# A transformer block on one core: new order of stages, scores in two pieces, first norm's weights applied in the copy

## Chip, cores and metric

One core of one Trainium2 chip. The metric is the device time of one execution in microseconds (us), as the median of several runs. The engines are called TensorE (PE, with its weight loads as PEld), VectorE (DVE), ScalarE (ACT), GpSimd (POOL) and SyncE (SP, which here only issues DMAs).

## What is computed

The input is 4 sequences of 2048 tokens with 256 features, float32. Cut to what matters:

```python
x  = x + attn(layernorm(x))            # attn is a pre-norm block of its own
x  = x + experts(layernorm(x))

attn(q_x): xn = ln1(q_x)               # mean, variance, times ln1_w, plus ln1_b
  q, k, v = xn @ wq + bq, xn @ wk + bk, xn @ wv + bv    # 16 heads of 16
  fq, fk = elu(q) + 1, elu(k) + 1
  kv  = einsum("bhnd,bhne->bnde", fk, v)     # per token: over the HEADS
  qkv = einsum("bhnd,bnde->bhne", fq, kv)
  qk  = einsum("bhnd,bnd->bhn", fq, fk.sum(heads))
  x   = q_x + (qkv / (qk + 1e-6)) @ wo + bo
  x   = x + gelu(ln2(x) @ fc_w + fc_b) @ proj_w + proj_b    # 256 -> 1024 -> 256

experts(x): gates from the mean of a sequence (top 2 of 8, softmax)
  out = sum over chosen e of gate[e] * gelu(x @ expert_w[e].T + expert_b[e])
```

The attention mixes the 16 heads of one token with each other, not tokens. The kernel does it as scores between all heads of 4 tokens at a time (a 64x64 block), times a mask that keeps pairs of the same token, times the values.

## The kernel before

The work is cut into 16 **tiles** of 512 tokens, four to a sequence. No engine is scheduled by a planner: the function `iterations` (line 58) yields, for iteration 0 to 23, a list of **stage** names, and each engine walks the same lists and issues, in that order, its own part of each stage. So one list sets five in-order queues at once, and an instruction that waits holds back everything behind it on its engine, DMA issues included. `LAG` (line 43) gives how many iterations behind the newest tile a stage works. In the steady state an iteration handles five different tiles.

The stages that matter, by iteration i:

- `L`: SP loads tile i. `DS`, `D1`: DVE statistics and normalisation of tile i into `xhat` (the reciprocal root is POOL's, line 418). `X`: PE transposes `xhat` (L827) and ACT copies it to `xhT` (L458). `DV`, `DQ`, `DK`: PE multiplies with the value, query and key weights (L871, eight matmuls each); ACT takes exp and relu (L480, L481), DVE joins them to features (L650), SP stores them (L326). Values are stored by ACT's own DMA queue (L473), which waits first until the values of the tile before have been read back.
- `VL`: SP reads the values of tile i-1 back in another layout, 16 DMAs (L339); `VT` transposes them (PE L879, ACT L488). `K0`, `K1`: SP reads queries and keys of the first and of the second half of a tile, 8 DMAs each (L351). `B0`: PE scores of the first half (L890, 128 matmuls of 16x64), and DVE's mask (L657).
- `M1` to `M4`: four rounds of the 256-1024-256 network of tile i-3 (up-projection L933, gelu L503 and L504, rest L670, down-projection L917) merged with attention of tile i-2. `M1` multiplies the scores of the first half with the values (L902), and ACT evicts to `ot` (L511). `M2` holds the scores of the second half, `M3` their product with the values. `M2` and `M4` on SP each do two things: they store half of `ot` to `scratch_nd` (L357), wait for that to land, and load it back as numerator and denominator (`nd`, L362). `B1` to `B4` are the same without the network, `C1` to `C4` the network alone.
- `N0`, `N`: DVE divides the two halves (reciprocal L686), and `N` splits the result into `hT` (L696, L697). `A2`: PE output projection (L977, 24 matmuls), DVE adds and takes statistics (L707 and on). `R`: DVE normalises to `hn` (L596). `H`: PE transposes `hn` (L827) for the network; the copies are ACT L492 and DVE L677.
- `J7`, `JA`: last down-projection and its sum. `Y`, `YB`: the residual's part. `XS`, `XL`: SP stores and reloads the network's result. `F1`, `F3`: PE runs the two chosen experts (L839), `F4` joins them, `FX` is a branch for a third, `F2` transposes the sum (L1021), adds (L803) and stores (L380). `G`: the gate of a sequence, once in four tiles (L991).
- Head only: `W1` folds the first norm's weight and bias into the query, key and value weights (PE L846, DVE L622 and L625), and ACT begins only when that is done. `WS` folds the second norm's and splits the weights of three products into two float32r parts each (DVE, lines 630 to 642).

`TAIL` (line 46) is the second part of an iteration from 7 on, `MERGED` (line 49) its first. Iterations 3 to 6 use `EARLY` (line 50), whose second part already has `A2` ahead of `DK`:

```python
TAIL = ["DV", "DQ", "DK", "A2", "F1", "R", "F3", "F4", "SA", "H", "B0", "FX", "F2"]
MERGED = ["L", "XS", "VL", "K0", "M1", "J2", "Y", "M2", "K1", "DS", "Z", "M3", "D1", "M4", "N0"]
```

## Time and profile before

| what | value |
|---|---|
| median of 3 runs | 1129.65 us (1126.64 to 1133.05) |
| the profiled execution's own time | 1129.7 us |
| its span in the trace | 1127.8 us |
| PE busy | 974.4 us (86%), 12232 matmuls |
| DVE, ACT, POOL busy | 58%, 43%, 16% |
| mean granted PE clock | 0.916 of full speed |
| chain that ended last | PE 48%, SP's queue 13%, DVE 12%, issue 12%, DMA 10% |

PE is busy most of the span, but not evenly: in 40 slices its busy tenths are 5 7 5 4 7 at the start and 9 or 8 through the middle. The clock column shows 1.0 as full speed and 0.5 as half: 2.4 and 1.2 GHz. A matmul that runs at half clock counts as busy for twice as long, so a busy PE can still lose time.

### The profile page before, as it was taken

What the parts mean: (1) busy time and instruction counts of PE and PEld (TensorE: products, weight loads), DVE (VectorE), ACT (ScalarE), POOL (GpSimd) and SP (SyncE); (2) the same over time, 40 slices, a digit from 0 to 9 for tenths busy, and PEclk for the clock granted to TensorE, in tenths of its full rate; (3) what the DMA queues carried; (4) which work ended last, traced back from release to release, by engine and by line L of the source; (5) the groups of instructions that cost most, each with busy time, mean ns of one, the idle gap of its engine ahead of it and who ended that gap; (6) DMA issues with size and microseconds to landing.
All of it is one profiled execution on the core that took longest, in us unless ns stands there. A gap on an engine that the chain in (4) does not pass through costs nothing.

```text
span 1127.8 us, 29248 instructions
## 1 busy us (share of the span) xinstructions
PE 974.4 (86%) x12232; PEld 736.0 (65%) x12232; DVE 654.8 (58%) x1564; ACT 486.3 (43%) x770; POOL 185.2 (16%) x113
## 2 busy tenths in 40 slices
PE   5754798989898899999999899999999899797966
PEld 3342676767676758685777668586866768585723
DVE  1263566667665665765656766656656664657433
ACT  1413354535353444545363454445453455152422
POOL 1020121212121211212111211212111210202000
PEclk9858798989898899999998999989999999798989
DMA  4556255454545435546364545546364544241123
GB/s 179 114 96 136 42 124 99 119 103 115 100 119 101 115 76 141 114 114 140 96 147 91 137 86 120 108 116 138 94 140 94 134 98 98 53 122 39 38 74 113
DMA packets 360343, 120.88 MB, mean 107 GB/s; under 512 B 325520, under 2 KB 342160, under 8 KB 359952
## 3 DMA queue, kind: packets, MB, share of 16 engines
q1 hardware_dynamic: 353552, 108.47, 42.9%
q10 hardware_dynamic: 6656, 10.50, 2.7%
q8 instruction: 98, 1.61, 0.6%
q14 instruction: 37, 0.30, 0.1%
HBM read 60.20 MB, written 58.72 MB: 105 GB/s over the span
## 4 chain that ended last, share of the span: by engine, by line
PE 48%; SPq 13%; DVE 12%; issue 12%; DMA 10%; POOL 3%; ACT 1%; ACTq 1%; DVEq 0%; POOLq 0%
PE pw L933 10%; PE pj L917 8%; DMA scratch_nd<-ot 5%; SPq L339 5%; PE ps L871 5%; PE ps L890 5%; SPq L351 5%; PE pw L839 4%; PE pj L839 4%; PE ps L977 3%; DMA nd<-scratch_nd 3%; PE ps L902 2%; PE pw L871 2%; DVE nd L686 2%; SPq L362 2%
## 5 line engine op out<-in xcount | busy, mean ns | idle before, releaser
L933 PE MATMUL pw<-hT,w_fc 128*128 128x512 f32 x768 | 219.1, 428 | 9.6 <-DVE hT L677 9.6
L917 PE MATMUL pj<-w_pj,hidden 128*128 128x256 f32 x1536 | 215.6, 291 | 2.7 <-DVE hidden L670 2.7
L917 PEld LDWEIGHTS pj<-w_pj,hidden 128*128 128x128 f32 x1536 | 203.9, 196 | 14.1 <-DVE hidden L670 3.7
L670 DVE TENSOR_TENSOR hidden<-xhT,hidden 128x512 fp32r<-128x512 f32 x128 | 88.5, 691 | 206.8 <-ACT hidden L504 206.0
L503 ACT ACTIVATE xhT<-pw,col 128x512 f32<-128x512 f32 x128 | 88.0, 688 | 252.9 <-PE pw L933 251.6
L933 PEld LDWEIGHTS pw<-hT,w_fc 128*128 128x128 f32 x768 | 151.1, 208 | 42.5 <-DVE hT L677 11.5
L871 PE MATMUL ps<-xhT,w_qkv 128*128 128x512 f32 x256 | 125.5, 636 | 3.4 <-ACT xhT L458 3.2
L657 DVE TENSOR_TENSOR am<-ps,mask 128x512 f32<-128x512 f32 x128 | 79.4, 683 | 41.5 <-PE ps L890 41.5
L890 PE MATMUL ps<-kq 16*64 16x64 f32 x4096 | 81.9, 311 | 21.9 <-issue 19.7
L890 PEld LDWEIGHTS ps<-kq 16*64 16x64 f32 x4096 | 74.4, 209 | 35.5 <-issue 35.5
L686 DVE RECIPROCAL nd<-nd 128x256 f32<-128x256 f32 x32 | 56.0, 1749 | 64.1 <-DMA nd<-scratch_nd 64.1
L871 PEld LDWEIGHTS ps<-xhT,w_qkv 128*128 128x128 f32 x256 | 51.2, 207 | 62.0 <-issue 57.4
L504 ACT ACTIVATE hidden<-pw,col 128x512 fp32r<-128x512 f32 x128 | 87.5, 684 | 0.0
L511 ACT ACTIVATE ot<-ps,den_eps 128x512 f32<-128x512 f32 x64 | 69.7, 1197 | 38.3 <-PE ps L902 37.5
L977 PE MATMUL ps<-w_o,hT 128*128 128x256 f32 x384 | 55.9, 306 | 34.0 <-DVE hT L697 34.0
L977 PEld LDWEIGHTS ps<-w_o,hT 128*128 128x128 f32 x384 | 51.6, 207 | 45.5 <-DVE hT L697 26.9
L650 DVE SCALAR_TENSOR_TENSOR fqk<-elu 128x512 f32<-128x512 f32 x64 | 42.9, 688 | 54.1 <-ACT elu L481 54.1
L424 POOL TENSOR_TENSOR x<-x,row 128x1024 f32<-128x1024 f32 x16 | 37.6, 2351 | 222.3 <-DVE x_sb L722 219.5
L839 PE MATMUL pw<-zT,w_e 128*128 128x512 f32 x128 | 59.6, 609 | 8.4 <-DMA b_e<-in_eb 7.7
L418 POOL TENSOR_TENSOR rs<-var,mhalf 128x8 f32<-128x8 f32 x16 | 27.8, 1740 | 215.1 <-DVE var L611 209.5
L839 PE MATMUL pj<-zT,w_e 128*128 128x512 f32 x128 | 57.8, 594 | 5.5 <-DVE out_sb L803 5.5
L871 PE MATMUL pw<-xhT,w_qkv 128*128 128x512 f32 x128 | 57.8, 594 | 0.7 <-ACT vb L488 0.7
(109 smaller groups left out, 1187.9 us busy)
## 6 DMA issues: line engine op xcount, KB each, us to landing
scratch_nd<-ot SPq DMA_DIRECT2D x32, 512.0 KB, 4.1
nd<-scratch_nd SPq DMA_DIRECT2D x96, 128.0 KB, 2.7
x_sb<-in_x SPq DMA_DIRECT2D x16, 512.0 KB, 5.9
scratch_v<-feat_v ACTq DMA_DIRECT2D x16, 512.0 KB, 2.9
scratch_q<-fqk SPq DMA_DIRECT2D x32, 256.0 KB, 3.6
scratch_k<-fqk SPq DMA_DIRECT2D x32, 256.0 KB, 4.7
vd<-scratch_v SPq DMA_DIRECT2D x256, 32.0 KB
kq<-scratch_q SPq DMA_DIRECT2D x128, 64.0 KB, 2.7
```

The source lines that it names most:

```text
L503: nc.scalar.activation(gelub[:, u], pw[u], ACT.Gelu, bias=b_fc[:, m:m + 1])
L504: nc.scalar.activation(hidden[:, m % SLOTS, 0], pw[u], ACT.Gelu, bias=b_fc[:, m:m + 1]).then_inc(S[f"pw_free{u}"], 1)
L511: nc.scalar.activation(dst[:, r // 2, v], src, ACT.Identity, bias=den_eps[:, :]).then_inc(S[f"sa_free{v}"], 1)
L657: last = nc.vector.tensor_tensor(am[:, j].rearrange("p (k n) -> p k n", n=BLOCK), ps[:, j].rearrange("p (k n) -> p k n", n=BLOCK), mask[:, ...
L670: nc.vector.tensor_tensor(hidden[:, m % SLOTS, 1], gelub[:, u], hidden[:, m % SLOTS, 0].bitcast(f32), ALU.subtract).then_inc(S["rest_ready ...
L686: link(nc.vector.reciprocal(d, d))
L839: last = nc.tensor.matmul(bank, w[:, c, P * m:P * (m + 1)], zT[:, p.t % RING, c], start=(c == 0), stop=(c == NC - 1))
L871: last = nc.tensor.matmul(bank, w_qkv[:, j // NC, c, P * (j % NC):P * (j % NC + 1)], xhT[:, c], start=(c == 0), stop=(c == NC - 1))
L890: last = nc.tensor.matmul(ps[BLOCK * v:BLOCK * (v + 1), j, BLOCK * k:BLOCK * (k + 1)], kd[rows, b, cols], qd[rows, b, cols], start=True, s ...
L917: last = nc.tensor.matmul(pj[u][:, D * s:D * (s + 1)], hidden[:, m % SLOTS, a, lo:lo + P], w_pj[:, b, m], start=(m == 0 and n == 0 and s = ...
L933: last = nc.tensor.matmul(pw[bank], w_fc[:, b, c, P * m:P * (m + 1)], hT[:, a, c], start=(n == 0), stop=(n == len(order) - 1))
L977: last = nc.tensor.matmul(sb2[u][:, D * s:D * (s + 1)], attnT[:, a, c, lo:lo + P], w_o[:, b, c], start=(c == 0 and n == 0), stop=(c == NC ...
```

## The change

Five edits, all in the order of the work but one:

1. **First norm.** `W1` is gone. ACT's copy of `xhT` applies `ln1_w` as scale and `ln1_b` as bias, per partition.
2. **First tiles.** Iterations 0 to 2 have new lists: statistics of tile 1 and 2, and `D1`, run an iteration earlier; `WS` comes ahead of `DV` of tile 1; `K0` comes ahead of `VL`.
3. **Scores in two pieces.** `scores(b)` becomes `scores(b, part)` of 64 matmuls each. `B0` is split in `B0` and `B8`, with `H` and `F3` between them in iterations 7 to 15; in `M2` the pieces stand ahead of and behind the down-projection.
4. **SP.** Store and reload of `ot` are stages of their own: `NS0`, `NL0`, `NS1`, `NL1`. `VL` moves behind `NS0`, `K0` behind `NL0`, `K1` behind `NL1`.
5. **Tail.** `A2` moves between `DQ` and `DK`, `R` ahead of `F1`, `H` (norm's transposes) between `F1` and `F3`.

```diff
-TAIL = ["DV", "DQ", "DK", "A2", "F1", "R", "F3", "F4", "SA", "H", "B0", "FX", "F2"]
+TAIL = ["DV", "DQ", "A2", "DK", "R", "F1", "B0", "H", "F3", "F4", "SA", "B8", "FX", "F2"]
...
-MERGED = ["L", "XS", "VL", "K0", "M1", "J2", "Y", "M2", "K1", "DS", "Z", "M3", "D1", "M4", "N0"]
-EARLY = ["L", "VL", "K0", "M1", "Y", "M2", "K1", "DS", "M3", "D1", "M4", "N0", "X", "J7", "JA", "YB", "VT", "N",
-         "DV", "DQ", "A2", "R", "DK", "SA", "B0", "H"]
+MERGED = ["L", "XS", "M1", "J2", "Y", "NS0", "VL", "M2", "NL0", "K0", "DS", "Z", "M3", "NS1", "D1", "M4", "NL1", "N0", "K1"]
+EARLY = ["L", "M1", "Y", "NS0", "VL", "M2", "NL0", "K0", "DS", "M3", "NS1", "D1", "M4", "NL1", "N0", "K1", "X", "J7", "JA", "YB",
+         "VT", "N", "DV", "DQ", "A2", "R", "DK", "SA", "B0", "B8", "H"]
...
-    yield 0, ["DS:0", "L:1", "D1", "W1", "X", "DV", "DQ", "DK"]
-    yield 1, ["DS", "D1", "VL", "K0", "K1", "X", "DV", "DQ", "DK", "L:2", "WS", "VT", "B0"]
-    yield 2, ["VL", "K0", "DS", "D1", "Y", "B1", "X", "DV", "B2", "K1", "DQ", "B3", "B4", "N0", "VT", "DK", "YB", "N",
-              "A2", "R", "SA", "B0", "H"]
+    yield 0, ["DS:0", "L:1", "D1", "X", "DV", "DS:1", "DQ", "L:2", "D1:1", "DK"]
+    yield 1, ["X", "K0", "WS", "VL", "DV", "DQ", "DS:2", "DK", "D1:2", "B0", "B8", "VT", "K1"]
+    yield 2, ["K0", "VL", "Y", "B1", "NS0", "X", "DV", "B2", "NL0", "DQ", "B3", "NS1", "VT", "NL1", "N0", "K1",
+              "DK", "YB", "N", "A2", "R", "SA", "B0", "B8", "H"]
...
-                if p.stage in ("B2", "M2", "B4", "M4"):
-                    half = int(p.stage[1]) // 2 - 1
+                if p.stage in ("NS0", "NS1", "NL0", "NL1"):
+                    half = int(p.stage[2])
                     part = slice(HALF * half, HALF * (half + 1))
+                if p.stage in ("NS0", "NS1"):
                     for u in range(2):
                         wait(f"sa_free{u}", at(f"sa_free{u}"))
                     sp.dma_start(nd_dram.rearrange("j e h t -> (j e) h t")[:, :, part], ot[:, :, part]).then_inc(S["nd_out"], 16)
+                if p.stage in ("NL0", "NL1"):
                     wait("attnT_ready", at("attnT_ready"))
-                    wait("nd_out", at("nd_out", 16))
+                    wait("nd_out", at("nd_out"))
...
-            act.wait_ge(fold_done, 1)
+            act.wait_ge(w_in[1], 16)
...
-                        nc.scalar.activation(xhT[:, c], sa[c], ACT.Identity).then_inc(S[f"sa_free{c}"], 1)
+                        nc.scalar.activation(xhT[:, c], sa[c], ACT.Identity, scale=ln1w[:, c:c + 1],
+                                             bias=ln1b[:, c:c + 1]).then_inc(S[f"sa_free{c}"], 1)
...
-                def scores(b):
+                def scores(b, part):
 
                     wait("sc_free", at("sc_free"))
-                    for k in range(KG):
+                    for k in range(KG // 2 * part, KG // 2 * (part + 1)):
...
-                    last.then_inc(S["sc_full"], 1)
+                    if part:
+                        last.then_inc(S["sc_full"], 1)
...
-                        scores(1)
+                        scores(1, 0)
                     if "C" in parts and r:
                         wait("rest_ready", at("rest_ready"))
                         down(2 * r - 1)
+                    if "B" in parts and r == 1:
+                        scores(1, 1)
```

What this moves, first on PE in the tail of an iteration without a gate (iterations 8 to 10 and the like). Names are those of the stages above: `ps<-xhT` is `DV` or `DK`, `pw<-xhT` is `DQ`, `w_o` is `A2`, `pw<-zT` and `pj<-zT` are the experts, `hn` is `H`, `kq` are scores (rows count pairs of matmuls). Before:

```order
L871 MATMUL ps<-xhT,w_qkv 128x512 x4
L871 MATMUL pw<-xhT,w_qkv 128x512 x4
L871 MATMUL ps<-xhT,w_qkv 128x512 x4
L977 MATMUL ps<-w_o,hT 128x256 x24
L839 MATMUL pw<-zT,w_e 128x512 x4
L839 MATMUL pj<-zT,w_e 128x512 x4
L827 MATMUL pw<-ident,hn 128x128 x8
L890 MATMUL ps<-kq 64x64 x64
```

And now:

```order
L859 MATMUL ps<-xhT,w_qkv 128x512 x4
L859 MATMUL pw<-xhT,w_qkv 128x512 x4
L970 MATMUL ps<-w_o,hT 128x256 x24
L859 MATMUL ps<-xhT,w_qkv 128x512 x4
L832 MATMUL pw<-zT,w_e 128x512 x4
L878 MATMUL ps<-kq 64x64 x32
L820 MATMUL pw<-ident,hn 128x128 x8
L832 MATMUL pj<-zT,w_e 128x512 x4
L878 MATMUL ps<-kq 64x64 x32
```

The output projection moved ahead of the keys, and a block of scores became two, with transposes and an expert between.

On SP, the same iteration, from the load of a tile to the reload of `XL`; `vd` is `VL`, `kq` is `K0` and then `K1`, `scratch_nd<-ot` the store and `nd<-scratch_nd` the reload. Before:

```order
L312 DMA x_sb<-in_x 128x4x256
L316 DMA scratch_x<-x_sb 128x1024
L339 DMA vd<-scratch_v 16x16x32 x16
L351 DMA kq<-scratch_q 16x2x512 x4
L351 DMA kq<-scratch_k 16x2x512 x4
L357 DMA scratch_nd<-ot 2048x1x64
L362 DMA nd<-scratch_nd 128x4x64 x3
L351 DMA kq<-scratch_q 16x2x512 x4
L351 DMA kq<-scratch_k 16x2x512 x4
L357 DMA scratch_nd<-ot 2048x1x64
L362 DMA nd<-scratch_nd 128x4x64 x3
```

And now:

```order
L311 DMA x_sb<-in_x 128x4x256
L315 DMA scratch_x<-x_sb 128x1024
L357 DMA scratch_nd<-ot 2048x1x64
L338 DMA vd<-scratch_v 16x16x32 x16
L363 DMA nd<-scratch_nd 128x4x64 x3
L350 DMA kq<-scratch_q 16x2x512 x4
L350 DMA kq<-scratch_k 16x2x512 x4
L357 DMA scratch_nd<-ot 2048x1x64
L363 DMA nd<-scratch_nd 128x4x64 x3
L350 DMA kq<-scratch_q 16x2x512 x4
L350 DMA kq<-scratch_k 16x2x512 x4
```

The 16 value loads now stand between the first store and its reload, and the second half's queries and keys behind the second reload.

On SP in iterations 0 and 1, from the query features of tile 0 to the stores of tile 1. Before:

```order
L326 DMA scratch_q<-fqk 128x16x32 x2
L326 DMA scratch_k<-fqk 128x16x32 x2
L339 DMA vd<-scratch_v 16x16x32 x16
L351 DMA kq<-scratch_q 16x2x512 x4
L351 DMA kq<-scratch_k 16x2x512 x4
L351 DMA kq<-scratch_q 16x2x512 x4
L351 DMA kq<-scratch_k 16x2x512 x4
L326 DMA scratch_q<-fqk 128x16x32 x2
```

And now:

```order
L325 DMA scratch_q<-fqk 128x16x32 x2
L311 DMA x_sb<-in_x 128x4x256
L325 DMA scratch_k<-fqk 128x16x32 x2
L350 DMA kq<-scratch_q 16x2x512 x4
L350 DMA kq<-scratch_k 16x2x512 x4
L338 DMA vd<-scratch_v 16x16x32 x16
L325 DMA scratch_q<-fqk 128x16x32 x2
```

Tile 0's values are now loaded behind its first queries and keys, and its second half's behind the stores of tile 1.

## Rows read from the trace of the kernel before

**Rows 1.** What PE waited for, 360 to 965 us (total us, times, longest).

```profile
PE ps L890 <- issue: 10.5, 10, 2.0
...
PE ps L977 <- DVE hT L697: 6.8, 4, 2.6
```

**Rows 2.** Busy time by stretch: PE, PEld, DVE, ACT, POOL, granted clock, DMA share, GB/s.

```profile
0.00:130.00 130.00, 75.43 (x842) 49.38 (x843) 51.07 (x122) 33.00 (x51) 16.72 (x24) 0.79 0.51 120
...
360.00:965.00 605.00, 565.15 (x7271) 430.96 (x7269) 377.64 (x923) 289.13 (x461) 106.26 (x57) 0.95 0.50 114
```

**Rows 3.** Timeline of PE, head: start, duration, instruction, idle before and its releaser.

```profile
16.24 1.97 PE L827 MATMUL ps<-ident,xhat 128*128 128x128 f32 x8 [1.93 <-DVE w_qkv L625]
...
39.52 1.97 PE L827 MATMUL ps<-ident,xhat 128*128 128x128 f32 x8 [7.31 <-DVE xhat L596]
...
115.73 4.55 PE L977 MATMUL ps<-w_o,hT 128*128 128x256 f32 x24 [15.76 <-DVE hT L697]
```

**Rows 4.** Timeline of SP's queue, head.

```profile
34.81 11.44 SPq L339 DMA_DIRECT2D vd<-scratch_v  x16
...
102.15 1.69 SPq L357 DMA_DIRECT2D scratch_nd<-ot  x1
107.45 1.46 SPq L362 DMA_DIRECT2D nd<-scratch_nd  x3
```

**Rows 5.** Timeline of ACT and of DVE, head.

```profile
49.26 0.45 ACTq L473 DMA_DIRECT2D scratch_v<-feat_v  x1
...
95.00 2.05 ACT L511 ACTIVATE ot<-ps,den_eps 128x512 f32<-128x512 f32 x2 [0.89 <-PE ps L902]
...
111.05 1.75 DVE L686 RECIPROCAL nd<-nd 128x256 f32<-128x256 f32 x1 [7.83 <-DMA nd<-scratch_nd]
```

**Rows 6.** Timeline of PE, one iteration without a gate.

```profile
545.69 1.68 PE L917 MATMUL pj<-w_pj,hidden 128*128 128x256 f32 x12
...
548.70 0.75 PE L890 MATMUL ps<-kq 16*64 16x64 f32 x23
550.99 2.10 PE L890 MATMUL ps<-kq 16*64 16x64 f32 x105 [1.54 <-issue]
553.02 2.93 PE L917 MATMUL pj<-w_pj,hidden 128*128 128x256 f32 x12
...
585.73 3.24 PE L977 MATMUL ps<-w_o,hT 128*128 128x256 f32 x24
```

**Rows 7.** Timeline of PE: the first up-projections of two iterations.

```profile
480.37 3.04 PE L933 MATMUL pw<-hT,w_fc 128*128 128x512 f32 x12
...
601.02 4.26 PE L933 MATMUL pw<-hT,w_fc 128*128 128x512 f32 x12
```

**Rows 8.** Timeline of SP's queue, the iteration of rows 6.

```profile
545.77 13.03 SPq L339 DMA_DIRECT2D vd<-scratch_v  x16
...
567.46 1.48 SPq L362 DMA_DIRECT2D nd<-scratch_nd  x3
...
573.09 0.56 SPq L357 DMA_DIRECT2D scratch_nd<-ot  x1
577.23 1.48 SPq L362 DMA_DIRECT2D nd<-scratch_nd  x3
```

**Rows 9.** Timeline of ACT and of DVE, the same iteration.

```profile
545.74 2.22 ACT L511 ACTIVATE ot<-ps,den_eps 128x512 f32<-128x512 f32 x2
...
581.14 1.75 DVE L686 RECIPROCAL nd<-nd 128x256 f32<-128x256 f32 x1 [5.06 <-DMA nd<-scratch_nd]
```

**Rows 10.** The page: a DMA queue's packets and MB, and an issue's median us to landing.

```profile
q8 instruction: 98, 1.61, 0.6%
...
scratch_k<-fqk SPq DMA_DIRECT2D x32, 256.0 KB, 4.7
```

**Rows 11.** Timeline of SP's queue in iteration 4.

```profile
183.40 11.96 SPq L339 DMA_DIRECT2D vd<-scratch_v  x16
...
211.13 0.56 SPq L357 DMA_DIRECT2D scratch_nd<-ot  x1
```

**Rows 12.** Timeline of PE, iteration 16.

```profile
970.77 5.31 PE L977 MATMUL ps<-w_o,hT 128*128 128x256 f32 x24 [5.37 <-DVE hT L697]
```

More of the change, by code:

```diff
@@ L660, in masked @@
                     last.then_inc(S["sc_free"], 1)
[L662 removed]
+                if p.stage == "B8":
                     masked()
[L664 removed]
+                elif p.stage[0] in "BCM" and p.stage not in ("B0", "B8"):
                     parts, r = of_round(p.stage)
@@ L811, in _ @@
             wait = waiter(pe)
-            for n in range(3):
+            for n in range(2):
                 pe.wait_ge(w_in[n], 16)
@@ L841, in expert @@
                     return last
-                if p.stage == "W1":
-                    for n in range(3 * NC):
-                        for c in range(NC):
-                            last = nc.tensor.matmul(pw[0][:, n:n + 1], w_qkv[:, n // NC, c, P * (n % NC):P * (n % NC + 1)],
-                                                    ln1b[:, c:c + 1], start=(c == 0), stop=(c == NC - 1))
-                    last.then_inc(S["pw_full0"], 1)
-                    pe.wait_ge(fold_done, 1)
                 if p.stage == "WS":
@@ L940, in run @@
                     empty("sb")
-                    scores(0)
-                elif p.stage[0] in "BCM":
+                    scores(0, 0)
+                elif p.stage == "B8":
+                    scores(0, 1)
+                elif p.stage[0] in "BCM" and p.stage not in ("B0", "B8"):
                     parts, r = of_round(p.stage)
```

39 lines of the change are left out of this document (15 added, 24 removed).

## The prediction

> **What bounds the kernel now.** I read the stretches first, then PE's waits, then the timelines of PE and of SP's queue. The stretches [rows 2] show two kernels in one. In the first 130 us PE is busy for 75 us at a clock of 0.79: the head is a chain of waits. From 360 to 965 us, where nine of the iterations with the long tail run, PE is busy for 565 of 605 us: there PE is the bound, and only what makes PE idle or slow can give time. That is three things. It waits 10.5 us in the middle of blocks of scores, put down to "issue", and 6.8 us ahead of the output projection for DVE's split `hT` [rows 1]. And the clock averages 0.95, so PE stands at the lower level (1.2 GHz) for 0.05 x 2 x 605, about 60 us, which costs at most half, 30 us [rows 2]. Where it falls is seen in one iteration [rows 6]: 23 matmuls of scores, 1.54 us of nothing, 105 more, and then a down-projection that takes 2.93 us where the one in front took 1.68. So a block of scores, 16 rows of the array and a hole in it, drops the clock for what follows. The first up-projection behind the other block of scores shows it too: 4.26 us against 3.04 [rows 7].
>
> **Head.** Today PE computes the bias fold, DVE scales the weights, and the first transposes start at 16.24 us after waiting 1.93 for it [rows 3]; DVE had `xhat` at 13.4. Without the fold they start there, and all of tile 0 comes 2.7 us earlier. The copies of `xhT` get a scale and a bias. I cost that at 0.1 us each, since ACT's copies with a bias take 0.69 us and those without 0.60; from iteration 3 on the down-projection and the value transposes hide them. The 7.31 us for tile 1's `xhat` [rows 3] go too, since its statistics now run under tile 0's products.
>
> But SP's order decides how much is kept. Key features of tile 0 are stored at 31.6 and land 4.7 us later [rows 10], 36.3. `K0` now stands in front and waits for that; its eight issues take 3.8 us, then `VL` takes 11.4 [rows 4], to 51.5 against 46.3 today, landed at about 54.2. ACT's store of tile 1's values waits for it, in order, and today is issued at 49.26 without waiting [rows 5]. So ACT's exp and relu of tile 1 begin at 54.9, 5 us later than today, not 10 earlier. DVE splits the weights under this stall (9.5 us of work that today delays the first mask to 69.3 us), so the mask can run at 63.3, the first product with values at 65.8 (today 71.9), and tile 2's transposes at 69 (today 77). The same happens once more. Tile 1's keys are stored by 62.1 and land at 66.8; `K1` and `K0` take 7.5 us, `VL` 11.4, landed at 88.4, where ACT is waiting again. It evicts the second `ot` at 91.6 to 93.6, against 95.0 to 97.1 [rows 5]. The store follows at 94.1, against 102.15, as `K1` no longer stands in front. The reload is 5.3 us behind it as today (107.45) [rows 4], at 99.4, and DVE's last division starts at 103.0 in place of 111.05 [rows 5]. The output projection starts at 107.7 instead of 115.73 [rows 3]. **Head: 8 us.** If ACT's stall cost nothing it would be 14; if the crowded queue stretches both `VL`, 3.
>
> **SP in every iteration.** The chain is: `ot` evicted, store, reload, division, output projection. Today `ot` is ready at 547.96 [rows 9], but the store waits behind `VL` and `K0`, and the second reload at 577.23 stands behind the first round trip and `K1` [rows 8]. Now: `ot` 547.96, store 0.55, `VL` 12.4 to 13.0, reload 1.5, `K0` 3.8, store 0.6, 4.15 to land (573.65 to 577.23 today), reload 1.5, 2.4 to the division, 4.5 to `hT`. That is 579.5 to 580.1, against 585.7 today: 5 to 6 us earlier. In iterations 3 to 6 less is won, for `VL` starts at 183.40 today [rows 11], and behind the store it would be at about 193. Added up as above, the second store comes at 210.4 to 211.6, against 211.13 [rows 11]: no gain, at most 1 us lost in each; their tails do not change. I put 0, with -3 as the end. In iteration 16 today's `VL` also starts early, 5.3 us ahead of `ot`, so 2.5 us of the 5.37 us wait [rows 12] go, and part of the low clock behind it (5.31 us for what takes 3.1 to 3.2): **3 us**, between 0 and 6.
>
> **Tail.** `A2` moves ahead of `DK` on PE, so it wants `hT` 3.4 us earlier. PE today takes from 545.69 to 585.73 [rows 6]; less the hole (1.54), the slow down-projection (1.3) and `DK` (3.4) that is 33.8, so `A2` could start at 579.5. SP's chain gives 579.5 to 580.1. The two arrive together: of the 6.8 us of waits [rows 1] I keep half a microsecond in each of nine iterations: **2 us** won, between -5 and 6.8. What is late next is nothing on PE. DVE has the statistics of `A2` at about 588.2, POOL the root at 589.5, DVE the key features at 591.1 and `hn` at 592.5; PE comes to `H` at 593.8 behind `F1` and half the scores. ACT frees the second `pw` bank of `F1` at 593.3, half a microsecond ahead of that. `F2` needs the experts' sum at 599.75 and the branch lets PE through at 600.2. These covers are thin; if each is missed by 0.5 us in nine iterations it costs 4 us per cover. Keys are stored up to 2 us later, read 30 us after that.
>
> **Scores in pieces.** It adds no matmul: 2.41 us of scores become twice 1.2. The clock: behind `M2`'s scores eight down-projections and what follows lose about 1.5 us each, behind the tail's block five up-projections about 1.3 with the transposes in front: 18 us of the 30 in rows 2. With a down-projection, or `H` and an expert, between pieces of 1.2 us, I expect the clock to hold in two of three: **13 us**, between 0 and 18. The holes: instructions come as their own DMA traffic, 98 packets of 1.61 MB, so about 16.4 KB each [rows 10]. The hole stands in `M2` after 56, 40, 23, 7 matmuls of the block in following iterations, and then 114, 97, 81, 64: a fixed step, as the edge of such a packet would walk. DMA is busy there with `F2`'s store, `L` and `XS`. Where the edge falls in the second piece it now comes 1.6 us later and the hole of 1.5 is covered; in the first piece nothing changes. Half: **5 us**, between 0 and 10.5.
>
> The Trainium skill ("Runtime: NRT & Kernel Launch", Instruction fetch mechanics) says that instructions are fetched in blocks of 16 KiB, ahead of use, and that this is hidden because engines dispatch more slowly than blocks fill. The packet size agrees; that it is hidden does not fit 10.5 us of holes. By that rule the pieces would gain no hole and the sum below would be 5 us smaller.
>
> **Sum.** 8 + 3 + 2 + 13 + 5 = 31 us. Against the profiled execution's own 1129.7 us (the median is 1129.65, so nothing is to be corrected) that is 1098.7: **1099 us**.
>
> **Rivals.** (a) *The pieces do nothing*: the clock drops as before because both pieces are still thin work close together, and the holes only move. For it: in rows 6 only 23 matmuls stood before the hole, and a hole can still fall in the first piece. Against: of two up-projections behind the same block, one held its clock [rows 7], so it is near the edge. Then 8 + 3 + 2: 1117 us; if the waits also cost a little, 1120. (b) *Everything comes off*: head 14, clock 18, holes 10.5, waits 4, iteration 16 5: 51 us, 1078 us. (c) *Slower*: `VL` in front of the first reload delays the second reload on SP. If it were issued no earlier than now relative to `ot`, `A2` would wait 3.4 us in nine iterations, 31 us, and lose clock behind each wait as in rows 12, some 1.5 us each, 13 more, and the pieces' 18 would be eaten by the same waits. 1129.7 - 8 + 44 - 18 = 1148 us. It decides from the point where `VL` or the landing takes over 5.5 us more than in rows 8. Against: the added times leave 5 us of room. (d) *The order does not reach the time*: the head is given back, since iteration 3 waits for the same store chain, and the rest as in (a): 1127 us.
>
> **How the numbers follow.** Forecast 0.54 (its own range 1087 to 1111), (a) 0.23, (b) 0.12, (c) 0.05, (d) 0.06. A measurement of this kernel tells about 0.5%, 5.6 us, from no change. Faster by more than that: forecast, (b), (a): 0.89. Within: (d), 0.06. Slower: (c), 0.05. The range takes in (a) and the near half of (b): 1081 to 1120 us.
>
> **What would show it.** In the profile after: first transposes at 13.4 us; ACT's second value store at 54 and its third at 88; the head's output projection at 108; in the middle stretch a clock of 0.97 or more, "issue" ahead of scores at about 5 us, and the output projection waiting under 6 us in all. The second reload should stand 5 us earlier behind `ot`. A wait of over 2 us ahead of each output projection, or a clock still at 0.95, proves me wrong.

## The result and the profile after

| | median, us | range, us | runs |
|---|---|---|---|
| before | 1127.21 | 1122.08 to 1133.28 | 15 |
| after | 1119.64 | 1114.89 to 1126.25 | 15 |

The ratio is 0.9928, 95% interval 0.9905 to 0.9951: **faster by 7.6 us, 0.7%**. The forecast was 31 us. The time lies inside the range, a fraction of a microsecond from its upper end, and next to rival (a), 1117 to 1120 us. The direction was right, the size four times too large.

The profiled execution took 1116.99 us, 12.7 less than the profiled one of before. That pair flatters the change: before's was above the median of its 15 runs and after's below its own. So where I set the two traces beside each other below, the terms add up to about 13 us, not 7.6. The granted clock says the same: 0.935 in after's profiled execution is the highest of its 15, whose median is 0.928.

The page of after, the shares of the chain that ended last, by engine and by line:

```profile
PE 44%; SPq 20%; issue 11%; DVE 11%; DMA 9%; ACT 3%; POOL 2%; ACTq 0%; DVEq 0%; POOLq 0%
SPq L338 13%; PE pw L922 10%; PE ps L859 6%; PE pj L906 5%; PE pw L832 4%; PE pj L832 4%; DMA scratch_nd<-ot 4%; PE ps L970 4%; SPq L350 4%; PE ps L878 3%; DMA nd<-scratch_nd 3%; PE ps L891 3%; SPq L363 2%; DVE nd L679 2%; PE pj L1014 1%
```

SP's queue was 13% of the chain before and is 20% now, and the line of the value loads alone (L338) is 13%. This is the first sign of what went wrong: the chain that sets the end runs more through a queue of DMA issues than before.

The second stretch of [rows 2], now (PE, PEld, DVE, ACT, POOL, clock, DMA share, GB/s):

```profile
360.00:965.00 605.00, 564.06 (x7390) 425.17 (x7375) 386.94 (x930) 291.80 (x460) 104.60 (x58) 0.97 0.51 115
```

The clock rose from 0.95 to 0.97, as forecast. A fixed stretch doesn't hold the same work in both, so here it is from the first up-projection of iteration 7 to that of iteration 16, first before, then after, with 6853 matmuls in each:

```profile
352.62:925.21 572.59, 534.01 (x6853) 405.69 (x6853) 360.74 (x885) 273.26 (x435) 100.68 (x54) 0.94 0.50 114
```

```profile
349.36:918.35 568.99, 531.22 (x6853) 398.19 (x6853) 363.06 (x885) 277.65 (x435) 98.48 (x54) 0.96 0.51 116
```

PE's busy time fell by 2.8 us only, although the clock rose, and its idle time by 0.8 only (38.6 to 37.8), although the holes shrank. So something took back most of each: the pieces themselves the one, longer waits the other, as is shown below. What PE waited for from 360 to 965 us (total us, times, longest), against [rows 1]:

```profile
PE ps L970 <- DVE hT L690: 11.8, 7, 3.1
...
PE ps L878 <- issue: 4.4, 3, 2.3
```

The holes in the scores fell from 10.5 to 4.4 us. The output projection's wait for `hT` rose from 6.8 to 11.8 us, where I had forecast 4.5. Of the 11.8, 0.9 are iteration 16's, whose wait of before lies outside this stretch; in the nine iterations the wait rose from 6.8 to 10.9.

**Where the 13 us came from.** I took, in both traces, the start of the first up-projection of an iteration, and the differences between such marks:

| part | start of the part's last mark, before and after | gained, us | forecast |
|---|---|---|---|
| head, to iteration 3 | 129.42, 123.45 | 6.0 | 8 |
| iterations 3 to 6 | 352.62, 349.36 | -2.7 | 0 |
| iterations 7 to 15 | 925.21, 918.35 | 3.6 | 20 |
| iteration 16 | 985.23, 971.0 | 7.4 | 3 |
| 17 to the end | | -1.3 | 0 |

The nine iterations with the long tail hold the miss: 3.6 us in place of 20 (2 waits, 13 clock, 5 holes).

**Head.** PE, ACT and SP in after, timelines (start, duration, instruction, idle before and its releaser), against [rows 3 to 5]:

```profile
13.31 1.94 PE L820 MATMUL ps<-ident,xhat 128*128 128x128 f32 x8 [13.31 <-DVE xhat L598]
...
109.77 4.54 PE L970 MATMUL ps<-w_o,hT 128*128 128x256 f32 x24 [12.28 <-DVE hT L690]
123.45 4.50 PE L922 MATMUL pw<-hT,w_fc 128*128 128x512 f32 x12 [1.75 <-DVE hT L670]
```

```profile
52.73 0.38 ACTq L475 DMA_DIRECT2D scratch_v<-feat_v  x1
53.21 0.69 ACT L482 ACTIVATE elu<-pw,col 128x512 f32<-128x512 f32 x1 [10.39 <-DMA vd<-scratch_v]
...
87.80 0.37 ACTq L475 DMA_DIRECT2D scratch_v<-feat_v  x1
```

```profile
36.86 1.73 SPq L350 DMA_DIRECT2D kq<-scratch_q  x4
...
40.63 10.43 SPq L338 DMA_DIRECT2D vd<-scratch_v  x16
...
95.60 1.51 SPq L357 DMA_DIRECT2D scratch_nd<-ot  x1
```

The chain of the prediction is there, each link within three microseconds: transposes at 13.3 (forecast 13.4), ACT's second value store at 52.7 behind a stall of 10.39 us for `VL` (54), its third at 87.8 (88), the second store of `ot` at 95.6 (94.1), the output projection at 109.8 (107.7).

**One iteration of the middle.** SP's queue, against [rows 8]:

```profile
425.35 0.56 SPq L357 DMA_DIRECT2D scratch_nd<-ot  x1
426.02 14.51 SPq L338 DMA_DIRECT2D vd<-scratch_v  x16
440.63 1.64 SPq L363 DMA_DIRECT2D nd<-scratch_nd  x3
442.38 2.60 SPq L350 DMA_DIRECT2D kq<-scratch_q  x4
445.03 1.82 SPq L350 DMA_DIRECT2D kq<-scratch_k  x4
446.95 0.57 SPq L357 DMA_DIRECT2D scratch_nd<-ot  x1
451.46 1.48 SPq L363 DMA_DIRECT2D nd<-scratch_nd  x3
```

`ot` was evicted at 425.3. The second reload is issued 26.2 us later. Before it was 29.3 (547.96 to 577.23), and my sum of terms gave 23 to 23.6. So SP's chain is 3.1 us shorter, not 5 to 6. The mean of iterations 8 to 15 says the same, 29.0 before and 26.0 now; in iteration 7, the first of the nine, it even grew, from 22.1 to 25.7. `VL` took 14.51 us here and 14.4 in the mean of ten iterations, where I had put 12.4 to 13.0 (before's mean in iterations 8 to 15 is 12.9). The chain of waits, split into single issues, shows which (start, us):

```profile
426.02 2.36 SPq L338
...
429.09 1.89 SPq L338
```

Three of the sixteen loads took 2.36, 1.89 and (at 437.54) 1.68 us, the others 0.61 each. The longest single value load of the stretch is 1.94 us before and 4.15 us after (issues of that line: shortest, median, longest in ns):

```profile
L338 SPq DMA_DIRECT2D vd<-scratch_v x160: 532/609/4150, 359.4 to 938.1; - x160
```

It is mostly the first load that is long: 2.4 to 4.2 us in iterations 8 to 15. A store in front doesn't explain that by itself. In iterations 4 to 7 the first load stands behind the same store and takes 0.9 to 1.2 us, and before the change it stood right behind the store of `XS` (`scratch_x<-x_sb`), which is as large, and took 0.6. What more it takes was not found.

And this is what PE met at the end of it, in this iteration and in the next one:

```profile
460.40 4.62 PE L970 MATMUL ps<-w_o,hT 128*128 128x256 f32 x24 [3.13 <-DVE hT L690]
...
521.63 3.11 PE L970 MATMUL ps<-w_o,hT 128*128 128x256 f32 x24 [1.21 <-DVE hT L690]
```

Behind a wait of 3.13 us the same 24 matmuls take 4.62 us, behind one of 1.21 they take 3.11. So this wait was paid about one and a half times. Not every wait is: in iteration 3 one of 3.13 us is followed by the same matmuls in 3.13.

**The pieces.** The scores of `M2` with the down-projection between the pieces, in after, and then the whole block in before, ahead of the same down-projection:

```profile
426.02 1.38 PE L878 MATMUL ps<-kq 16*64 16x64 f32 x64
427.33 1.68 PE L906 MATMUL pj<-w_pj,hidden 128*128 128x256 f32 x12
428.94 1.38 PE L878 MATMUL ps<-kq 16*64 16x64 f32 x64
430.25 1.67 PE L922 MATMUL pw<-hT,w_fc 128*128 128x512 f32 x6
```

```profile
933.87 2.41 PE L890 MATMUL ps<-kq 16*64 16x64 f32 x128
936.21 1.68 PE L917 MATMUL pj<-w_pj,hidden 128*128 128x256 f32 x12
937.72 1.56 PE L933 MATMUL pw<-hT,w_fc 128*128 128x512 f32 x6
```

From start to start, scores and down-projection take 1.31 + 1.61 + 1.31 = 4.23 us in pieces and 2.34 + 1.51 = 3.85 whole, both without a hole. Two pieces cost 0.38 us more than one block in `M2`. In the tail, from the start of `F1` to that of `F2`, it is 11.32 us (from 589.81) against 11.04 (from 588.80), with waits alike: 0.28 more. With nine of each that is about 6 us that the prediction did not have.

### The profile page after: what moved, and what is told of

Read it like the earlier page. It is cut to its first block, busy times and chain, and to the rows that moved or that the text cites. A ratio compares the mean times of both kernels' runs of the same rounds, so it can differ in the third digit from the quotient of the medians.

```text
span 1114.9 us, 29193 instructions
## 1 busy us (share of the span) xinstructions
PE 964.3 (86%) x12208; PEld 719.0 (64%) x12208; DVE 650.1 (58%) x1557; ACT 492.4 (44%) x770; POOL 184.3 (17%) x113
## 3 DMA queue, kind: packets, MB, share of 16 engines
q8 instruction: 98, 1.61, 0.6%
## 4 chain that ended last, share of the span: by engine, by line
PE 44%; SPq 20%; issue 11%; DVE 11%; DMA 9%; ACT 3%; POOL 2%; ACTq 0%; DVEq 0%; POOLq 0%
SPq L338 13%; PE pw L922 10%; PE ps L859 6%; PE pj L906 5%; PE pw L832 4%; PE pj L832 4%; DMA scratch_nd<-ot 4%; PE ps L970 4%; SPq L350 4%; PE ps L878 3%; DMA nd<-scratch_nd 3%; PE ps L891 3%; SPq L363 2%; DVE nd L679 2%; PE pj L1014 1%
## 5 line engine op out<-in xcount | busy, mean ns | idle before, releaser
L922 PE MATMUL pw<-hT,w_fc 128*128 128x512 f32 x768 | 214.6, 421 | 11.4 <-DVE hT L670 11.4
L906 PE MATMUL pj<-w_pj,hidden 128*128 128x256 f32 x1536 | 208.9, 285 | 3.8 <-DVE hidden L663 3.8
L906 PEld LDWEIGHTS pj<-w_pj,hidden 128*128 128x128 f32 x1536 | 197.7, 190 | 15.3 <-DVE hidden L663 5.0
L505 ACT ACTIVATE xhT<-pw,col 128x512 f32<-128x512 f32 x128 | 87.8, 686 | 232.3 <-PE pw L922 231.0
L922 PEld LDWEIGHTS pw<-hT,w_fc 128*128 128x128 f32 x768 | 145.3, 200 | 44.6 <-DVE hT L670 12.9
L878 PEld LDWEIGHTS ps<-kq 16*64 16x64 f32 x4096 | 77.5, 210 | 55.0 <-issue 53.2
L878 PE MATMUL ps<-kq 16*64 16x64 f32 x4096 | 88.3, 314 | 27.5 <-issue 16.3
L832 PE MATMUL pw<-zT,w_e 128*128 128x512 f32 x128 | 59.4, 607 | 8.4 <-DMA b_e<-in_eb 7.8
```

The lines of the kernel that those rows point to most:

```text
L505: nc.scalar.activation(gelub[:, u], pw[u], ACT.Gelu, bias=b_fc[:, m:m + 1])
L832: last = nc.tensor.matmul(bank, w[:, c, P * m:P * (m + 1)], zT[:, p.t % RING, c], start=(c == 0), stop=(c == NC - 1))
L878: last = nc.tensor.matmul(ps[BLOCK * v:BLOCK * (v + 1), j, BLOCK * k:BLOCK * (k + 1)], kd[rows, b, cols], qd[rows, b, cols], start=True, s ...
L906: last = nc.tensor.matmul(pj[u][:, D * s:D * (s + 1)], hidden[:, m % SLOTS, a, lo:lo + P], w_pj[:, b, m], start=(m == 0 and n == 0 and s = ...
L922: last = nc.tensor.matmul(pw[bank], w_fc[:, b, c, P * m:P * (m + 1)], hT[:, a, c], start=(n == 0), stop=(n == len(order) - 1))
```

## Experiments

Each is timed beside before on the same chip; ratios are to before. Where two variants are compared, after's ratio is 0.9928, and 0.001 is 1.1 us. Times are medians, rows are of one profiled execution, and that can lie off the median: it took 1130.80 us in experiment 2 and 1137.96 in experiment 6, the longest of twelve in both, and 1110.68 in experiment 3, second shortest of six.

### 1. The head alone

After with its edits 3 to 5 undone: only the lists of iterations 0 to 2 and the first norm's weights in the copy remain.

```diff
-TAIL = ["DV", "DQ", "A2", "DK", "R", "F1", "B0", "H", "F3", "F4", "SA", "B8", "FX", "F2"]
+TAIL = ["DV", "DQ", "DK", "A2", "F1", "R", "F3", "F4", "SA", "H", "B0", "B8", "FX", "F2"]
...
-MERGED = ["L", "XS", "M1", "J2", "Y", "NS0", "VL", "M2", "NL0", "K0", "DS", "Z", "M3", "NS1", "D1", "M4", "NL1", "N0", "K1"]
+MERGED = ["L", "XS", "VL", "K0", "M1", "J2", "Y", "M2", "NS0", "NL0", "K1", "DS", "Z", "M3", "D1", "M4", "NS1", "NL1", "N0"]
```

with `EARLY` and iterations 16 and 17 likewise, and the second piece of `M2` right behind the first.

> The changed kernel with edits 3 to 5 undone: scores in one block, the old tail, the old order on SP from iteration 3 on. What is left is the first norm in the copy and the new iterations 0 to 2. Theory A (the head's gain is real and is kept): the network of tile 0 starts 6 us earlier, as in the changed kernel (123.4 against 129.4 us), and the whole is 5 to 6 us faster than before, 1121 us. Theory B (later iterations wait for the same store chain and give it back): within 2 us of before, 1125 to 1129 us.

Measured: 1123.83 us, ratio 0.9984 (0.9959 to 1.0008). The first up-projection of iteration 3 starts at 124.15, 5.3 us ahead of before; at iteration 7 the lead is 3.6 us, at the end 2.2. The head is faster in itself and most of it is given back by the iterations behind it. Nearer B than A. That the store chain is what takes it back, as B has it, isn't shown: PE's waits for `hT` in iterations 3 to 6 add up to 4.7 us here and 4.4 before.

### 2. Both blocks of scores whole

```diff
-TAIL = ["DV", "DQ", "A2", "DK", "R", "F1", "B0", "H", "F3", "F4", "SA", "B8", "FX", "F2"]
+TAIL = ["DV", "DQ", "A2", "DK", "R", "F1", "H", "F3", "F4", "SA", "B0", "B8", "FX", "F2"]
...
                         scores(1, 0)
+                        scores(1, 1)
...
-                    if "B" in parts and r == 1:
-                        scores(1, 1)
```

> The changed kernel with both blocks of scores whole again, all else kept (in the tail the block stands behind the second expert). Theory A (pieces hold the clock and cover holes): the middle stretch falls back from a clock of 0.97 to 0.95 and 'issue' ahead of scores rises from 4 to about 10 us, less the 5 us that the pieces cost by themselves (two pieces take 2.62 us where one block took 2.35): 8 to 12 us slower than the changed kernel, 1128 to 1132 us. Theory B (pieces do next to nothing): 1118 to 1121 us.

Measured: 1125.69 us, 0.9977 (0.9952 to 1.0002). It lies between A and B. In the middle stretch the clock is 0.95 again, and two of PE's waits are:

```profile
PE ps L878 <- issue: 12.1, 8, 2.1
...
PE pw L820 <- ACT feat_v L545: 4.6, 9, 0.5
```

So holes and low clock are back, and the whole is worth 5.5 us in the time, not 18. Two things stand in the way of reading those 5.5 us as the worth of the pieces. With the tail's block whole, `H` stands right behind `F1` and waits half a microsecond for ACT in each of nine iterations, 4.6 us that after does not have and before had not either. And over all twelve executions the kernel's granted clock has a median of 0.927, next to after's 0.928 (before 0.917): in the median execution most of the clock's rise is there with whole blocks too.

### 3. The output projection back behind the keys

```diff
-TAIL = ["DV", "DQ", "A2", "DK", "R", "F1", "B0", "H", "F3", "F4", "SA", "B8", "FX", "F2"]
+TAIL = ["DV", "DQ", "DK", "A2", "R", "F1", "B0", "H", "F3", "F4", "SA", "B8", "FX", "F2"]
```

> The changed kernel with the output projection behind the keys again in iterations 7 to 15 (R still ahead of F1). Theory A (the output projection now stands ahead of its data, 11.8 us of waits in the middle stretch, with low clock behind them): the waits go to under 3 us and the time falls by 6 to 10 us to 1110 to 1114 us. Theory B (its place ahead of the keys is needed so that hn is ready for the transposes between the experts): PE waits at the transposes for hn instead, 1 to 2 us in each of nine iterations, 1120 to 1126 us.

Measured: 1117.55 us, 0.9915 (0.9886 to 0.9943), as after, between the two forecasts. PE's waits of this kernel, 360 to 965 us:

```profile
PE pw L820 <- DVE hn L598: 10.8, 10, 2.1
...
PE ps L970 <- DVE hT L690: 1.4, 1, 1.4
```

The wait for `hT` went from 11.8 to 1.4 us, and one of 10.8 us for `hn` stands ahead of the transposes instead. The place of the projection only says where PE waits for SP's chain. That the early place is worth anything here is not borne out.

### 4. SP's old order under the new rest

`MERGED`, `EARLY` and iterations 16 and 17 as in experiment 1; `TAIL`, pieces and head as in after.

> The changed kernel with SP's old order from iteration 3 on (values, first keys, store and reload, second keys, store and reload). Theory A (the new order brings the second reload forward, which the early output projection needs): PE waits 3 to 5 us ahead of it in each of nine iterations, 20 to 30 us slower than the changed kernel, 1140 us or more. Theory B (the new order gains nothing, as the value loads take 14 us in it in place of 12 to 13): within 3 us of the changed kernel, 1117 to 1123 us.

Measured: 1157.55 us, 1.0276 (1.0251 to 1.0301). PE's waits, 360 to 965 us:

```profile
PE ps L970 <- DVE hT L690: 38.2, 6, 8.5
```

More than theory A had. With the output projection early, SP's new order is worth 39 us. The early output projection of edit 5 can't be had without edit 4.

### 5 and 6. One block whole, the other in pieces

Experiment 5 undoes the pieces in `M2` only (the last two hunks of experiment 2), experiment 6 those of the tail only (its first hunk).

> The changed kernel with only M2's scores in one block again (the tail's block stays in two pieces around the transposes and an expert). Theory A (the clock is what pieces give, and eight of the thirteen low stretches stood behind M2): most of the 5.5 us between the changed kernel and the one with both blocks whole is lost, 4 us, 1123 to 1125 us. Theory B (the tail's pieces carry it, M2's only cost their 0.4 us per iteration): no slower than the changed kernel, 1116 to 1120 us.

> The changed kernel with only the tail's scores in one block again, behind the second expert; M2's stay in pieces. Theory A: 1 to 2 us slower than the changed kernel, 1119 to 1122 us. Theory B: 5 us slower, 1123 to 1126 us.

Measured: with `M2` whole 1122.11 us, 0.9957 (0.9936 to 0.9978), holes 12.4 us, clock 0.96. With the tail's block whole 1127.54 us, 1.0000 (0.9974 to 1.0025). The waits of the latter:

```profile
PE ps L970 <- DVE hT L690: 13.0, 6, 3.9
...
PE ps L878 <- issue: 5.6, 4, 2.0
```

The holes go with `M2`'s pieces (12.4 and 12.1 us without them, 5.6 and 4.4 with, the tail's block whole or cut). What else goes with which is seen in three parts of PE's timeline, added up over iterations 7 to 15 (us): from the start of `M2`'s scores to the up-projection behind its down-projection, with the idle time in it; the first up-projection behind the tail; and the output projection with its wait.

| | `M2`'s part | idle in it | first up-projection, and how many of nine took over 3.7 | output projection: wait, run |
|---|---|---|---|---|
| before, both whole | 55.7 | 9.8 | 32.6, 5 | 6.8, 30.5 |
| experiment 2, both whole | 59.4 | 12.1 | 29.7, 3 | 8.0, 30.2 |
| experiment 6, `M2` in pieces | 49.0 | 6.7 | 30.4, 3 | 13.0, 36.0 |
| experiment 5, tail in pieces | 56.5 | 12.4 | 27.6, 1 | 8.2, 28.7 |
| after, both in pieces | 46.6 | 5.5 | 28.1, 1 | 10.9, 31.5 |

`M2`'s pieces shorten their part by some 10 us, their own cost included, and about half of it is not idle time but clock. The tail's pieces hold the clock of the up-projection behind them: in the eight further traces with both in pieces none or one of nine is over 3.7 us. In those eight `M2`'s part takes 48.3 to 52.7 us, so after's 46.6 flatters the pieces. And the last column shows where the gain goes. From experiment 5 to after the output projection, with its wait, takes 5.5 us more, and of 9.9 us there are 4.6 left at the marks. From 2 to 6 it takes 10.8 us more, and nothing is left. In the time `M2`'s pieces are worth 0.3% where the tail is in pieces, and cost 0.2% where it is whole, which is within the intervals; the tail's are worth 0.7% where `M2` is in pieces, and 0.2%, again within the intervals, where it is whole. Experiment 6 also has the 4.6 us of waits at `H` that experiment 2 has, so the tail's pieces and the place of `H` are not told apart. Experiment 5 fits its theory A, and experiment 6 cost more than either of its theories allowed: I had expected the two to add.

### 7. A second buffer for the values

Tile 1's store of values waits in the head until tile 0's have been read. With two buffers it needn't.

```diff
-        v_dram = nc.dram_tensor("scratch_v", (D, T), f32, kind="Internal").ap()
+        v_dram = nc.dram_tensor("scratch_v", (2, D, T), f32, kind="Internal").ap()
...
-                    wait("v_in", at("v_in"))
+                    wait("v_in", at("v_in", -64 * NQ))
```

Load and store take `v_dram[p.t % 2]`.

> The changed kernel with two buffers in DRAM for the values, so that ACT's store of a tile's values waits for the read-back of the tile before the last: it takes away the two stalls of ACT in the head (10.4 and 7 us). Theory A (ACT's stall is on the head's chain, through the exp and relu behind it): the output projection of tile 0 starts 4 to 6 us earlier than the 109.8 us of the changed kernel. Whether it is kept to the end: theory A says yes, 1114 us; theory C (the head's gain is given back, as 6 us became 1.5 in the kernel with the head alone) says under 2 us of it, 1117 to 1120 us. If the stall is not on the chain, the output projection stays at 109 to 110 us.

Measured: 1116.84 us, 0.9912 (0.9881 to 0.9943), not to be told from after. ACT's stall is gone, and the head's output projection, which ended a wait for `hT` in after at 109.77, is here:

```profile
106.86 5.35 PE L970 MATMUL ps<-w_o,hT 128*128 128x256 f32 x24 [16.96 <-DVE hT L690]
```

2.9 us earlier, not 4 to 6. ACT evicts the second `ot` 7.6 us earlier (84.92 against 92.51), but SP issues its store only 3.2 us earlier (92.45 against 95.60): most of the gain ends at SP's queue, which is the head's limit.

### 8. `K0` into the landing of the second store

In after SP waits about 4 us between the second store and its reload with nothing to do, and `K0`, 4.5 us in the iteration shown and 4.0 in the mean of nine, stands in front of the store.

```diff
-MERGED = ["L", "XS", "M1", "J2", "Y", "NS0", "VL", "M2", "NL0", "K0", "DS", "Z", "M3", "NS1", "D1", "M4", "NL1", "N0", "K1"]
+MERGED = ["L", "XS", "M1", "J2", "Y", "NS0", "VL", "M2", "NL0", "DS", "Z", "M3", "NS1", "K0", "D1", "M4", "NL1", "N0", "K1"]
```

and so in `EARLY` and iteration 16.

> The changed kernel with the loads of the first half's queries and keys (3.8 us of issue on SP) moved from ahead of the second store to behind it, where SP waits 4.2 us for the store to land anyway. Theory A (the output projection waits for SP's chain, 11.8 us in the middle stretch): the second reload comes 3 to 4 us earlier behind the first ot, the waits go to under 2 us, and the time falls by 8 to 12 us to 1108 to 1112 us. Theory B (DVE's own order, with the division behind the network's sum, is the next limit right behind it): under 4 us, 1116 us or more.

Measured: 1109.67 us, 0.9837 (0.9807 to 0.9867), 10 us under after. SP's queue in this kernel:

```profile
439.42 0.56 SPq L357 DMA_DIRECT2D scratch_nd<-ot  x1
440.09 4.39 SPq L350 DMA_DIRECT2D kq<-scratch_q  x4
444.52 1.82 SPq L350 DMA_DIRECT2D kq<-scratch_k  x4
446.44 1.82 SPq L363 DMA_DIRECT2D nd<-scratch_nd  x3
```

From the first store (421.93) to the second reload it is 24.5 us, in after 26.1. `K0` got longer (four issues of queries in 4.39 us in place of 2.60, and 3.2 to 4.4 in all ten iterations, where after has 1.84 in seven), so only 1.6 of 4.5 us are won here, 1.8 in the mean of iterations 8 to 15; the wait ahead of the output projection falls from 11.8 to 7.2 us, not under 2 as theory A had, though the time is A's. A change to SP's queue alone gives more than the whole change under study did: in the new order the queue is a limit.

### 9. SP's old order with the output projection late

Experiments 3 and 4 together, to learn what SP's order is worth where `A2` is not early.

> The changed kernel with both: SP's old order from iteration 3 on and the output projection behind the keys. With the changed kernel, the one with the late projection and the one with the old order it makes a square. Theory A (SP's order is worth what the early projection asks of it): the 37 to 39 us that the old order costs with the early projection shrink to 5 to 15 us, that is 1123 to 1133 us here. Theory B (the old order is bad in itself, because first keys ahead of the store delay the second reload past both places): still 30 us or more, 1148 us.

Measured: 1144.05 us, 1.0167 (1.0131 to 1.0203). Against experiment 3, which differs in SP's order alone, the new order is worth 28 us even so; and the early projection, on SP's old order, costs 12 us (ratios of experiment 4 and this one), where on the new order it costs nothing. I had expected SP's order to be worth much less here; theory B's 30 us is near. The pieces, `R` and `H` in their new places, with the old order on SP, thus cost some 20 us against experiment 1, which has neither. PE's wait for `hT` is 12.8 us here and there are 8.5 for `hn`. Why these moves ask so much more of the old order is argued, not shown: they take away work that lay in front of the waits.

### 10. The old head under the new rest

Lists of iterations 0 to 2 as in before, but without `W1`.

```diff
-    yield 0, ["DS:0", "L:1", "D1", "X", "DV", "DS:1", "DQ", "L:2", "D1:1", "DK"]
-    yield 1, ["X", "K0", "WS", "VL", "DV", "DQ", "DS:2", "DK", "D1:2", "B0", "B8", "VT", "K1"]
+    yield 0, ["DS:0", "L:1", "D1", "X", "DV", "DQ", "DK"]
+    yield 1, ["DS", "D1", "VL", "K0", "K1", "X", "DV", "DQ", "DK", "L:2", "WS", "VT", "B0", "B8"]
```

> The changed kernel with iterations 0 to 2 in the old order, without the fold of the first norm: what the new order of the first tiles gives by itself within the changed kernel. The transposes of tile 0 start at 13.3 us in both. Theory A (head gains are kept): the network of tile 0 starts at 126 to 127 us in place of 123.4 and the time is 3 us longer, 1122 us. Theory C (they are given back): within 1.5 us of the changed kernel.

Measured: 1121.21 us, 0.9963 (0.9934 to 0.9991). Iteration 3 starts its network at 126.56 against 123.45 in after. The ratio is 0.0035 above after's, 3.9 us, with intervals that overlap: the new lists of the head are worth some 4 us, and nothing can't be excluded. The fold's removal (129.42 to 126.56) is the other half of the head's 6 us.

### 11 and 12. Towards a better order

Experiment 11 takes 7 and 8 together and puts `VL` ahead of the first store in `EARLY` and in iteration 16, where `ot` comes late. Experiment 12 adds to it that in iterations 7 to 15 eight of the value loads are issued ahead of the first store and eight behind it:

```diff
-MERGED = ["L", "XS", "M1", "J2", "Y", "NS0", "VL", "M2", "NL0", "DS", "Z", "M3", "NS1", "K0", "D1", "M4", "NL1", "N0", "K1"]
+MERGED = ["L", "XS", "VA", "M1", "J2", "Y", "NS0", "VB", "M2", "NL0", "DS", "Z", "M3", "NS1", "K0", "D1", "M4", "NL1", "N0", "K1"]
...
-                    for j in range(NQ):
+                    for j in {"VL": range(NQ), "VA": range(NQ // 2), "VB": range(NQ // 2, NQ)}[p.stage]:
```

> The kernel with the first queries' and keys' loads in the gap of the second store, and three more edits: two DRAM buffers for values, and in iterations 3 to 6 and 16 all value loads ahead of the first store, as SP idles there for 8 us before the first ot is ready. Theory A (SP's chain sets the output projection in those iterations too): the waits ahead of it in iterations 3 to 6, 6.7 us in the changed kernel, go to 3, 1104 to 1107 us. Theory B (there DVE's division behind the network's sum is the limit): no better than 1109 to 1111 us.

> As the kernel before it in this call, and in iterations 7 to 15 half of the value loads are issued ahead of the first store of ot and half behind it: SP stands idle 2 to 4 us for ot there. Theory A (SP's issue time is what the output projection still waits for, 7.2 us in the middle stretch): the second reload comes 2 to 3 us earlier, the waits go to 2 us or less, 3 to 5 us faster than the kernel before. Theory B (half the loads ahead make the first store late by as much): no gain.

Measured: experiment 11 1107.56 us, 0.9832 (0.9799 to 0.9866), no clear gain over 8. Experiment 12 **1097.97 us, 0.9753 (0.9716 to 0.9790)**, 27 us under before and about 9 under 11, twice what I expected. Experiment 11 lies between its two theories. Experiment 12's queue of SP in one iteration, its waits and its chain:

```profile
415.77 6.07 SPq L338 DMA_DIRECT2D vd<-scratch_v  x8
421.93 0.73 SPq L357 DMA_DIRECT2D scratch_nd<-ot  x1
422.78 6.40 SPq L338 DMA_DIRECT2D vd<-scratch_v  x8
429.27 1.65 SPq L363 DMA_DIRECT2D nd<-scratch_nd  x3
433.55 0.56 SPq L357 DMA_DIRECT2D scratch_nd<-ot  x1
...
440.39 1.49 SPq L363 DMA_DIRECT2D nd<-scratch_nd  x3
```

```profile
PE ps L970 <- DVE hT L690: 4.9, 6, 0.9
```

```profile
PE 60%; DVE 15%; issue 10%; SPq 5%; DMA 3%; ACT 3%; POOL 2%; ACTq 1%; DVEq 0%; POOLq 0%
```

From the first store to the second reload it is now 18.5 us, but the store itself goes out 3.6 us after `ot` is ready at 418.3, as half of the value loads stand in front of it. From `ot` to the second reload it is 22.1 us, in the mean of iterations 8 to 15 22.6, against 26.0 in after and 24.3 in experiment 8. The longest wait ahead of the output projection is 0.9 us, and SP's queue falls from 20% of the chain to 5%. From iteration 7 to iteration 16:

```profile
345.08:903.51 558.43, 524.92 (x6852) 392.72 (x6853) 375.74 (x885) 277.81 (x435) 98.95 (x54) 0.98 0.55 118
```

Against after PE is idle for 4.3 us less and busy for 6.3 us less, and the clock is 0.98 in place of 0.96, with holes of 5.7 us. So the shorter queue gives back waits and clock. The reload now comes as early as the prediction had it for the change itself (23 to 23.6 us behind `ot`), and the time is about a microsecond from its 1099. That second agreement is partly luck: by the marks the gain against before is 9.7 us in the head, -2.1 in iterations 3 to 6, 14.2 in 7 to 15 and 8.3 in 16, where the prediction had 8, 0, 20 and 3, and the second buffer and the early values are not part of the change.

## Why the prediction was right in direction and wrong in size

- **What bounds the kernel** held for before. It failed to ask the question again for after: the 18 us that clock and holes were to free in the middle lie on PE, and SP's chain, which gives way by 3 us and not by 5 to 6, stands right behind: of the ten microseconds that `M2`'s pieces free, half or all come back at the output projection (experiments 5 and 6).
- **Head.** Each link came within three microseconds, and 6 us of 8 arrived at iteration 3. The failed step is that what the head wins is kept to the end: alone it is 2 us there (experiment 1), within after 0 to 4 for its lists (experiment 10). Rival (d) had this mechanism, and I gave it 0.06. The copies with scale and bias cost 0.18 us each and not 0.1 (mean 776 ns against 598). Whether this reached the time was not tried by itself.
- **SP in iterations 3 to 6.** Put at 0, end -3. It was -2.7. The waits ahead of the output projection rose from 4.4 to 6.7 us between 130 and 360 us, and four cuts in `M2` cost 1.5. But with SP's old order under the new rest (experiment 4) the four iterations take 225.6 us, with the new one 225.9, and before 223.2. So that SP's order is the loss, as the prediction had it, is not shown.
- **Iteration 16.** Put at 3, end 6; it gave 7.4. The projection that waited 5.37 us and took 5.31 [rows 12] now starts behind 0.92 and takes 3.08: 4.5 and 2.2 us. The wait went further than the 2.5 us that I had allowed. It is SP's order that does it: with the old one the iteration takes 58.8 and 59.1 us (experiments 4 and 9), with the new one 52.6 to 54.1 (2, 3, 5 to 7 and 10).
- **Tail and waits.** The term "I keep half a microsecond in each of nine iterations" failed: 10.9 us and not 4.5. The step is `VL` at 12.4 to 13.0 us. It was sized in its old place, and in its new one it takes 14.4. `K0` took 4.0 for 3.8. The sum was also made for one iteration and used for nine: in iteration 7 the old order had `VL` all but done (363.0) when `ot` was ready (361.9), and there the new order's second reload comes 3.6 us later behind `ot`. Rival (c) had the place and the point (5.5 us more than in the old rows); the queue went some 3 us of that way. Behind the two longest waits of the nine iterations (3.13 and 2.33 us) the low clock added 1.5 and 1.2 us, near what (c) had priced; behind the others nothing.
- **Clock.** 13 us forecast. 0.02 of 605 us, at twice the length and half the cost, is 12. The parts that the prediction had named give as much: the first up-projections are 4.5 us shorter, and `M2`'s part 9.1, of which 4.3 are idle time, while 3.4 were paid for the cuts: 4.5 and 8.2 of clock. So size and mechanism were right in this pair of traces. How much of it the pieces hold in the median execution is open, for with both blocks whole the whole kernel's clock has a median of 0.927, and in after 0.928.
- **Holes.** 5 us forecast, 6.1 found (10.5 to 4.4), and by `M2`'s pieces alone. The Trainium skill ("Runtime: NRT & Kernel Launch", Instruction fetch mechanics) has instruction fetch hidden by the pace of dispatch; by that no hole would have been there to lose. That they go with the place of the cut agrees with a cause in the stream of instructions, but which it is was not measured.
- **"It adds no matmul".** The step that failed outright. Number and size of the matmuls are the same, and each pair of pieces still takes 0.38 or 0.28 us more, 6 in the nine iterations; the prediction had this at nothing. Together: 12 clock and 6 holes, less 6 for the pieces, less 4 of waits for `hT` and 3 of waits elsewhere (`hidden`, `x`, the products with values), is 5, and the marks show 3.6. In the time the pieces are worth 5.5 us (experiment 2), a third of the 18 that I had given them, and of these up to 4.6 are the wait of `H` in that variant.
- **The range** of 1081 to 1120 held the time by 0.4 us, and by luck: it was set from 1129.7 us, and its upper end is 9.7 us below that, where the gain was 7.6. Before's median over 15 runs came out 2.4 us lower. Its upper end was rival (a) with "if the waits also cost a little"; the pieces did not do nothing, but what they cost and what SP's chain took back brought the sum there.

## What to carry over

When work moves on a queue that issues in order, price it in its new place: the same issues can take longer there (values 14.6 us for 12.9). Here the cheapest places for independent issues were the wait of a store for its landing, and the time before the store's data are ready. Measure the queue from the moment when the data are ready, not from the store. When a change frees time on the engine that is the bound, look for the chain that is next and how much slack it has, for no more than that can be had; here a second reload 3.4 us earlier behind `ot` in each of these iterations, with two small edits beside it, turned a gain of 7.6 us into one of 27. And a dense block that is cut in two is not free even if it holds the same instructions: measure from start to start.

## What was not expected of the hardware

- Value loads, 0.61 us each, whose first took 2.4 to 4.2 us behind a store of 512 KB in iterations 8 to 15, but 0.9 to 1.2 behind the same store in iterations 4 to 7, and 0.6 before the change behind another store of that size. All sixteen took 14.6 us in the mean of iterations 8 to 15, 12.9 before; half ahead of the store and half behind took 6.07 and 6.40 in the iteration shown, 13.5 in the mean. With `K0` behind a store, four issues took 4.39 us in place of 2.60. The cause was not found.
- Two pieces of 64 matmuls of 16x64 with a down-projection between take 0.38 us more than one of 128 in front of it: 1.31 us each against 2.34 for the whole, and the down-projection 1.61 against 1.51.
- The first up-projection behind the tail ran at a low clock in 5, 6, 3 and 3 of nine iterations where the block of scores was whole (before, experiments 1, 2 and 6), and in none or one where it was in two pieces with `H` and an expert between (ten traces), with about the same idle time in front of `F2` in both (mostly 0.7 us).
- The pieces in `M2` and those in the tail do not add. The holes go with the first, the clock with both, and the tail's are worth 0.7% or 0.2% by the state of the other.
